# One attention layer on one core: the second head's q and k as plain products, and another order for the front

## What is computed

```python
x = L0_attn_hidden_states                      # 1 x 1024 x 512, float32
x = x + attn(layernorm(x), wq, wkv, wo)        # 32 heads, causal
x = x + ffn(layernorm(x), k0, s0, k1, s1, k2, s2)

# attn: per head h, with 128 columns of q and k used
q = einsum('bsd,de->bse', x, wq).reshape(B, S, H, 192)
scores = einsum('bqhd,bkhd->bhqk', q[..., :128], k) * 192 ** -0.5
probs  = softmax(where(causal, scores, -1e30))
attn   = einsum('bhqk,bkhd->bqhd', probs, v);  return attn @ wo
```

## Time and profile before

| | before |
|---|---|
| time, median of 3 runs | 1162.95 us (1162.06 to 1163.11) |
| time of the profiled execution | 1162.55 us |
| its span in the trace | 1160.7 us |
| TensorE busy | 1102.2 us (95%) |
| VectorE busy | 899.0 us (77%) |
| ScalarE busy | 678.8 us (58%) |
| GpSimd busy | 676.9 us (58%) |

### The profile page before, as it was taken

The page is one execution under the profiler, slowest core; times in us unless marked ns, Lnnn a source line. Parts: engine busy times, 40 slices in busy tenths (PEclk is TensorE's granted clock), DMA queues, the critical chain, the costliest instruction groups (busy, mean ns, idle before and its releaser), DMA issues.

```text
span 1160.7 us, 22159 instructions
## 1 busy us (share of the span) xinstructions
PE 1102.2 (95%) x6217; PEld 655.3 (56%) x6217; DVE 899.0 (77%) x1799; ACT 678.8 (58%) x1335; POOL 676.9 (58%) x694
## 2 busy tenths in 40 slices
PE   4859999999999999999999999999999999999898
PEld 2515555556565555556555555656565555656577
DVE  6658777887878777787878787787877787787873
ACT  6545665656565565666565565566665565655453
POOL 2417576675656667665657657665657757665300
PEclk9979999999999999999999999999999999999999
DMA  4055664545554553555554553555454554555601
GB/s 154 4 118 90 112 104 89 114 104 118 111 122 83 123 104 75 124 105 122 111 111 81 119 114 73 120 115 124 97 116 87 109 113 85 118 99 99 105 1 73
DMA packets 367511, 117.33 MB, mean 101 GB/s; under 512 B 313088, under 2 KB 361344, under 8 KB 367488
## 3 DMA queue, kind: packets, MB, share of 16 engines
q1 hardware_dynamic: 367488, 117.05, 48.1%
HBM read 39.39 MB, written 2.12 MB: 36 GB/s over the span
## 4 chain that ended last, share of the span: by engine, by line
PE 66%; DVE 14%; issue 9%; ACT 6%; POOL 3%; DMA 1%; DVEq 1%; ACTq 0%; SPq 0%; POOLq 0%
PE psC L1094 38%; PE psS L1094 14%; PE psC L1218 13%; DVE p L966 3%; DVE attn L949 2%; ACT attn L725 2%; DVE qk L899 2%; ACT raw L671 1%; DVE psS L959 1%; POOL wqk L488 1%; DVE res L982 1%; ACT psS L703 1%; POOL wqk L485 1%; DMA wmax_rows<-wmax 1%; DVE bound L921 1%
## 5 line engine op out<-in xcount | busy, mean ns | idle before, releaser
L1094 PE MATMUL psC<-xb,wqk 128*128 128x512 f16 x1350 | 331.9, 385 | 18.6 <-POOL wqk L488 8.0
L703 ACT ACTIVATE psS<-psS,negmax 128x128 f32<-128x128 f32 (+7 forms) x256 | 182.8, 714 | 238.1 <-DVE negmax L959 235.9
L1094 PE MATMUL psC<-wos,attn 128*128 128x512 f32 x768 | 254.3, 442 | 12.5 <-DVE attn L949 8.9
L959 DVE CUSTOM_DVE_ANT_0 psS<-psS,mask,undo_qk 128x128 f32<-128x128 f32 (+7 forms) x256 | 209.2, 822 | 67.9 <-PE psS L1094 50.8
L966 DVE SCALAR_TENSOR_TENSOR p<-psS,p 128x128 f16<-128x128 f32 (+7 forms) x256 | 193.0, 754 | 72.8 <-ACT p L711 69.8
L1094 PE MATMUL psS<-qkT 128*128 128x512 f16 (+3 forms) x1152 | 231.4, 328 | 6.9 <-DVE p L966 4.8
L1094 PEld LDWEIGHTS psC<-xb,wqk 128*128 128x128 f16 x1350 | 124.6, 99 | 169.9 <-issue 26.3
L982 DVE SCALAR_TENSOR_TENSOR res<-psC,rinv,res 128x512 f32<-128x512 f32 x256 | 190.4, 744 | 11.2 <-DVE rinv L973 6.9
L1218 PE MATMUL psC<-pT,v 128*128 128x512 f16 (+3 forms) x1152 | 197.6, 326 | 0.2 <-DMA pT<-p 0.2
L536 POOL TENSOR_TENSOR qkT<-qk,qkT 128x512 f16<-128x512 f32 x124 | 141.5, 1157 | 92.7 <-ACT qkT L696 89.6
L1094 PE MATMUL psC<-wvs,xb 128*128 128x256 f16 x1536 | 189.0, 273 | 0.5 <-issue 0.4
(11 more groups left out here) (90 smaller groups left out, 934.0 us busy)
## 6 DMA issues: line engine op xcount, KB each, us to landing
raw<-in_L_attn_wkv SPq DMA_DIRECT2D x64, 256.0 KB, 3.3
raw<-in_L_attn_wq SPq DMA_DIRECT2D x32, 256.0 KB, 3.4
raw<-in_L_attn_wo SPq DMA_DIRECT2D x32, 256.0 KB, 3.2
pT<-p SPq DMA_TRANSPOSE x256, 4.3
wrow<-wmax_rows SPq DMA_DIRECT2D x45, 64.0 KB, 4.6
res<-in_L_attn_hidden_states SPq DMA_DIRECT2D x8, 256.0 KB, 5.6
out<-res SPq DMA_DIRECT2D x8, 256.0 KB, 2.0
raw<-in_L_ffn_k SPq DMA_DIRECT2D x3, 256.0 KB, 3.9
```

What stands on the lines that cost most here:

```text
L703: nc.scalar.activation(row, row, ACT.Exp, bias=negmax[:, n:n + 1], scale=-1.0, accum_out=rowsum[:, j % 2, n:n + 1]) \
L959: nc.vector.tensor_tensor_reduce(row, row, mask[:, S - width:S], undo_qk[:, j % 2:j % 2 + 1], 3e38, ALU.add, ALU.min, negmax[:, n:n + 1]). ...
L1094: last = nc.tensor.matmul(out_ap, w, x, start=k == 0, stop=k == len(terms) - 1)
```

## The change

Head 1 is now computed like head 0: steps y4 to y7 in place of x1 to x7. Its q and k weights get their own split (`split_plain`, two instructions) and lie in `S3` and `A11` of `wqk`; the sums, gathers, copy and splits of head 1 are gone. The waits count from head 2 on, and group 1 is written out, so the loop runs over groups 2 to 14. The first split of head 2 waits for y7 (`plain_done` 8). SyncE loads head 1's weights after tokens 4 to 7. The normalisation's scale is cut in two steps (`scale`, `rest`), `spread` 1 stands between y0 and y1, and the front's tables are new for all engines; the steady tables are unchanged.

```diff
-    spread2@2 y0@2 y1@2 turn4@2 turn5@2 turn6@2 turn7@2 v0@2 s0@2 v1@2 s1@2 v2@2 v3@2 y2@2 s2@2 y3@2 s3@2 x1@3 v4@2
-    s4@2 x2@3 v5@2 s5@2 x3@3 v6@2 s6@2 v7@2 s7@2""", "")
+    y0@2 spread1@2 y1@2 spread2@2 turn4@2 turn5@2 turn6@2 turn7@2 v0@2 v1@2 v2@2 s0@2 s1@2 y2@2 s2@2 s3@2 y3@2 v3@2
+    s4@2 v4@2 s5@2 y4@2 v5@2 s6@2 y5@2 s7@2 y6@2 v6@2 y7@2 v7@2""", "")
...
-    if h == 0 and (step[0] in ("x", "a", "snap", "sum", "qk", "mx", "sc", "r", "put", "get", "lqk", "lv") or step[0] == "wv" and step[2] == 2):
+    if h <= 1 and step[0] in ("x", "a", "snap", "sum", "qk", "wqk"):
+        return False
+    if h == 0 and (step[0] in ("mx", "sc", "r", "put", "get", "lqk", "lv") or step[0] == "wv" and step[2] == 2):
         return False
...
             body(-1)
             body(0)
-            with eng.Fori(1, NG - 1) as g:
+            body(1)
+            with eng.Fori(2, NG - 1) as g:
...
             load_values(sp, 0)
-            load_head(sp, 1, 1)
             for t in range(4, NT):
                 sp.dma_start(res[:, t, :], x_v[:, t, :]).then_inc(x_in[t], 16)
+            load_head(sp, 1, 1)
...
                 wait(pool, scaled[0], g, 1, j, 1)
-                if isinstance(g, int) and GH * g + j == 1:
+                if isinstance(g, int) and GH * g + j == 2:
+                    pool.wait_ge(plain_done, 8)
+                wait(pool, done["x"], g, 7, j, -5 - 14)
+                to = S3 if isinstance(g, int) and GH * g + j == 1 else A11
...
+            def split_plain(h):
+
+                to = (S2, A11)[h]
+                if h == 1:
                     pool.wait_ge(plain_done, 3)
...
             def plain_product_hi(n, bank):
+                h, to = n // 4, PLAIN[n % 4]
                 act.wait_ge(plain_done, n + 1)
+                if h == 1 and to != K0:
+                    act.wait_ge(done["s"], 4 if to == Q0 else 8)
...
             def plain_product(n, bank):
 
+                h, c, a = n // 4, n // 2 % 2, ((A11, S2), (S3, A11))[n // 4][n % 2]
+                pe.wait_ge(plain_lo if n % 2 else first_lo, h + 1)
```

More of the change, by code:

```diff
@@ L60 @@
     m7@1 o4@0 sc0@3 l6@1 a4@2 o5@0 a5@2 a6@2 a7@2 o6@0 l7@1 pv0@1 o7@0""", """
-    nlo0@2 nlo1@2 nlo2@2 nlo3@2 sc1@2 sc0@3 stat4@2 stat5@2 stat6@2 stat7@2 scale1@2 apply4@2 apply5@2 apply6@2
-    apply7@2 y0@2 y1@2 nlo4@2 nlo5@2 nlo6@2 nlo7@2 v0@2 m0@2 sum0@2 l0@2 v1@2 m1@2 sum1@2 l1@2 v2@2 v3@2 y2@2 m2@2
-    l2@2 y3@2 part0@2 m3@2 l3@2 part1@2 v4@2 m4@2 l4@2 a2@3 sum2@2 v5@2 m5@2 l5@2 sum3@2 part2@2 v6@2 m6@2 l6@2
-    part3@2 a3@3 v7@2 m7@2 sc0@4 l7@2""", "")
+    nlo0@2 nlo1@2 nlo2@2 nlo3@2 stat4@2 stat5@2 stat6@2 stat7@2 scale1@2 sc1@2 rest1@2 apply4@2 apply5@2 apply6@2
+    apply7@2 nlo4@2 nlo5@2 sc0@3 nlo6@2 y0@2 nlo7@2 y1@2 v0@2 m0@2 m1@2 l0@2 sum0@2 l1@2 sum1@2 m2@2 m3@2 v1@2 l2@2
+    y2@2 v2@2 y3@2 sum2@2 l3@2 m4@2 part0@2 m5@2 l4@2 v3@2 sum3@2 v4@2 l5@2 m6@2 y4@2 part1@2 m7@2 v5@2 l6@2 sc0@4
+    y5@2 part2@2 l7@2 v6@2 y6@2 v7@2 part3@2 y7@2""", "")
 SYNC_ORDERS = ("""
@@ L418, in loading_step @@
             if step == "lqk":
-                wait(q, sum_lo, g, 3, j, -6)
-                if isinstance(g, int) and GH * g + j == 2:
-                    q.wait_ge(first_lo, 1)
-                    q.wait_ge(plain_lo, 1)
+                wait(q, sum_lo, g, 3, j, -9)
+                if isinstance(g, int) and GH * g + j in (2, 3):
+                    q.wait_ge(first_lo, GH * g + j - 1)
+                    q.wait_ge(plain_lo, GH * g + j - 1)
                 load_head(q, g * GH + j, j % 2)
@@ L692, in qk_hi @@
             def qk_hi(g, j, n):
-                wait(act, gathered[LAST[n]], g, 1, j, 0)
+                wait(act, gathered[LAST[n]], g, 1, j, -1)
                 wait(act, done["s"], g, 8, j, {Q0: -4, Q1: 0, K0: -8, K1: 0}[n])
@@ L878, in gather @@
             def gather(g, j, n, bank):
-                wait(dve, done["x"], g, 7, j, n - 7)
+                wait(dve, done["x"], g, 7, j, n - 14)
                 if n < 4:
-                    wait(dve, x1_kept, g, 1, j, 0)
+                    wait(dve, x1_kept, g, 1, j, -1)
                 reused = {2: Q0, 3: Q1, 4: K0, 5: K1}.get(n)
@@ L887, in gather @@
                 for earlier in {4: (3,), 5: (4,), 6: (5,), 7: (5,)}.get(n, ()):
-                    wait(dve, gathered[earlier], g, 1, j, 0)
+                    wait(dve, gathered[earlier], g, 1, j, -1)
                 product = psC[:, bank, :]
@@ L989, in vector_step @@
                     norm_scale(n)
+                elif step == "rest":
+                    norm_rest(n)
                 elif step == "apply":
@@ L1064, in _ @@
             norm_scale(3)
+            norm_rest(3)
             ffn_lo(0)
@@ L1118, in spread, with bank_free @@
                                     ident[:, :]).then_inc(spread_done, 1)
-            def bank_free(g, before):
+            def bank_free(g, bank, before):
                 if before is None:
+                    if bank == 3:
+                        pe.wait_ge(bounded[0], 6)
+                        pe.wait_ge(bounded[1], 1)
                     return
@@ L1125, in bank_free @@
                 if kind == "x":
-                    wait(pe, x1_kept if n == 1 else gathered[n], g, 1, j, 0)
+                    wait(pe, x1_kept if n == 1 else gathered[n], g, 1, j, -1)
                 elif kind == "y":
-                    pe.wait_ge(qk_lo_done[PLAIN[n]], 1)
+                    pe.wait_ge(qk_lo_done[PLAIN[n % 4]], 1 + n // 4)
                 elif kind == "v":
@@ L1141, in product @@
                 elif n == 3:
-                    wait(pe, sum_lo, g, 3, j, 0)
-                if isinstance(g, int) and GH * g + j == 1 and b in T_USED:
+                    wait(pe, sum_lo, g, 3, j, -3)
+                if isinstance(g, int) and GH * g + j == 2 and b in T_USED:
                     pe.wait_ge(t_lo, T_USED[b])
@@ L1277, in ffn_chain @@
                 if before[0] != "ffn":
-                    bank_free(NG, before)
+                    bank_free(NG, bank, before)
                 else:
```

85 lines of the change are left out of this document (39 added, 46 removed).

## The result

| | before | after |
|---|---|---|
| time, median of 4 runs each, same chip | 1162.97 us (1162.06 to 1163.11) | 1142.87 us (1142.51 to 1143.02) |
| span in the trace | 1160.7 us | 1140.9 us |
| head 1's first score starts at | 86.25 us | 65.04 us |
| from there to the end of the span | 1074.5 us | 1075.9 us |

The ratio is 0.9828, with an interval of 0.9811 to 0.9845: 1.7% faster, 20.1 us. The forecast was 1140 with a range of 1135 to 1149. The direction and the mechanism are right, and the time is 2.9 us above the forecast. The last two rows of the table split that miss: the start came 21.2 us earlier instead of 23.0, and 1.4 us of it were lost behind the start. The profile has to explain both.

What follows compares the result with a forecast made beforehand. TensorE's front before head 1's first score was taken as the bound: that score moves from 86.25 to 63.2 us, a gain of 23.0, so 1162.55 becomes 1139.5, plus 0.4 to the median: 1140 us. Range 1135 to 1149.

Steps and rivals of the forecast that it cites:

- (1): TensorE's front: head 1's q and k from y4 to y7, 48 matmuls for 42, adding 1.3 us on the path.
- (2): Head 1's sums, gathers and x3's wait go; two splits precede y5; no head 1 score stands behind a chain of gathers.
- (3): SyncE's front: put at some 31.5 us, get at about 39; the pair stops costing anything.
- (4): Loading head 1's weights behind tokens 4 to 7 costs nothing; these tokens are normalised about 1.2 us earlier.
- (5): Group 1 written out in place of a loop pass: same instructions, price 0, bounds 0.34 us either way.
- (6): New wait before head 1's first score: GpSimd's split of head 2 waits for y7, so TensorE idles 1.0 us.
- The forward sum: From y0 at 18.0 us, 40.9 of TensorE work and 4.3 of waits put head 1's first score at 63.2.
- The backward sum: 86.25 - 15.4 idle - 7.9 clock + 1.3 + 1.0 = 65.2, less 1 to 2 gained before 50 us.
- A: Rival: VectorE falls behind, a new TensorE gap and lower clock give back 7.9 us, so 1148; chance 0.22.
- B: Rival: the predicted waits of 4.3 us in the front do not occur, 1135.5 us; chance 0.06 (below 1136).
- C: Rival: the lower clock stays from before score 0 until head 1 starts, at 91 us; time 1168, chance 0.04.
- D: Rival: the change does not move head 1's start, some unlisted chain holding it; 1164 us, chance 0.02.

Runs made afterwards that it cites:

- counts: The changed kernel with semaphores raised once at the start, so the loop's waits have their old constants; group 1 stays written out: 1141.58 us, ratio 0.9816.
- put_late: The changed kernel with SyncE's put and get among the transposes as before, and ScalarE's squares of head 2 behind part0: 1150.44 us, ratio 0.9900.
- load_back: The changed kernel with head 1's weights loaded before tokens 4 to 7 again: 1142.30 us, ratio 0.9824.
- counts_loop1: The changed kernel with the old wait constants, and group 1 a pass of the loop again: 1140.63 us, ratio 0.9806.
- before_sync: The kernel before with only SyncE's front reordered to t0, t1, put, t2, t3, get, t4: 1159.70 us, ratio 0.9977.
- before_fill: The kernel before with 26 unused identity transposes between the first spread and the tokens' first transposes: 1162.31 us, ratio 0.9993.

## Why the prediction was right, and where its sizes were off

**What bounds the kernel.** Right: TensorE's front, five gaps and the lower clock behind them. All of it went, and 19.8 of the 21.2 us by which the start moved arrived at the end. VectorE was to be busy nearly all of 30 to 62 us, and was busy 28.66 of the 32.

**(1) and (2).** Six matmuls more: x1356 on `xb,wqk`, at the predicted 0.216 each. No gather stands ahead of head 1's scores.

**(3) Put and get.** Put at 33.34 and get at 41.41, predicted 31.5 and 39. The put is late because y0 was (counts, with the fast y0, has it at 31.46). They are 8.1 apart, not 7.5, but no copy of ScalarE waited for a transpose. put_late shows the price if they stay: 7.6 us.

**(4) The load costs nothing.** Right (load_back). The squares came at 17.32, predicted about 17. But tokens 4 to 7 were to be normalised 1.2 us earlier, and that began at 25.01 us in after for 24.25 in before, since `rest` stood behind the spread's result and that behind the slow y0 (the 2.21 ahead of 23.24). In counts, whose y0 was fast, it began at 23.14, which is 1.1 earlier. TensorE waited 0.61 for it, as predicted.

**(5) Group 1 written out: 0.** The edit named there cost 0 (counts against counts_loop1). But the claim that went with it, the same instructions and a length of 1074.5 us from the first score on, failed. The diff also lowered the wait constants in the loop, and I read those lines as bookkeeping with no price. They cost 0.12 us a pass, 13 times, at a gather and at `undo_qk` on VectorE. The prediction named this growth as what would make it wrong, and it is where half of the miss lies.

**(6) The wait for head 2's weights.** 1.26 us, predicted 1.0 and 0.8 more for VectorE's subtraction beside it. It cost TensorE nothing: part3 began at 63.29, when the first of the two splits was done and the second nearly (62.45 + 1.16), these took 1.04 and 1.16 as always, and it was part3 that took 1.40 for its usual 1.22. The earlier meetings cost TensorE nothing either, the first one narrowly. The split for y4 took 1.88 for 1.04 at 42.40, beside VectorE's row of 42.17, so y4's weights were there at 45.51, 0.1 us before y4 began, where 0.4 was worked out. So the term of 1.2 was 0 (and the sum had counted its first half, although it calls it hidden). The rule of the Trainium skill (SBUF — State Buffer, Who interferes with whom) is that such a pair shares one set of ports, that the first holds it for its whole instruction and that the other blocks. The trace agrees, met part-way: in each pair the one that began second is longer by the time that the first still had to run, less 0.13 to 0.14 us. For the 42.40 row that is 0.98 left and 0.84 longer; for VectorE's 44.70 row, 0.81 left of the 44.36 split and 0.68 longer; for GpSimd's 45.48 row, 1.12 left of that and 0.98 longer; for part3, 0.32 and 0.18.

**The forward sum.** Predicted 63.2, measured 65.04:

| term | predicted | measured |
|---|---|---|
| y0 starts | 18.0 | 18.31 |
| TensorE's work at 2.4 GHz | 40.9 | 41.4 |
| y0 at the lower level | 0 | 2.0 |
| waits: transposes, score 3, score 4, head 2's weights | 3.1 | 0.61 + 0.72 + 0.39 + 1.26 = 3.0 |
| v0 waits for its weights | 0 | 0.36 |
| GpSimd beside VectorE | 1.2 | 0 |

The work is the 47.50 us of the first stretch less the 4.12 ahead of y0 and the 2.0; it is 0.5 more since the groups ahead of the five idle times last 0.15 longer, with nothing to overlap them, while the two spreads took 0.2 in place of 0.6.

The step that was mis-sized is the clock of y0. I put all of TensorE's work at 0.216 us a matmul, because in the trace before y0 ran so. There two small spreads stood at 16.75 and 18.85 us between the transposes and y0, with 1.62 us empty between them; the change moved both behind y0 and leaves 1.63 us empty. Whether that is why y0 was slow isn't shown: three kernels with the same instructions ahead had it fast, and two with the old order of spreads (before_sync, before_fill) had y0 and y1 slow. What is shown is that it can be lost and costs 2.0 us. The second error, 1.2 for GpSimd, went the other way and hid more than half of the first.

**The backward sum.** It gave 65.2 less 1 to 2; the 65.2 was the better figure, for the gains before 50 us were eaten by y0.

**The rivals.** A (a new gap and the lower clock): there is none behind y0, and VectorE held TensorE for 0.72 at most. put_late shows such a gap with another cause, the transposes, at 1150.44, where 1148 was put. That a gap of 2.51 brings the lower clock held in before and not in before_sync. B (no waits at all): the four waits came, each within 0.3 of its size. C and D: the clock was up from y1 on, and the start moved.

**From span to median.** I added 0.4 because the profiled execution before was 0.4 below its median; after, the profiled one (1143.02) is 0.15 above. And the time around the span was 2.1, not 1.85. The start's 1.8, the passes' 1.4 and this 0.3, less the 0.15 and the 0.4, make the 2.9.

## What to carry to other kernels

When a front is rewritten, look at every line of the steady loop that the diff touches, and cost even a changed constant in a wait: 0.12 us times the passes was as large as any of the small waits that I worked out one by one. A table of steps for a queue (here put and get among transposes) is worth 3 us or 8, depending on what stands beside it, so test it in both kernels. And treat the clock of the first matmuls behind an idle stretch as open, with both levels in the range, whatever one trace shows.
